# Expert results scattered to the tokens' places tile by tile, and register loads moved and taken one at a time

## What is computed

```python
logits = x @ gate_w + gate_b
probs = jax.nn.softmax(logits, axis=-1)
topv, topi = jax.lax.top_k(probs, K)
topv = topv / jnp.sum(topv, axis=-1, keepdims=True)
comb = jnp.sum(topv[..., None] * jax.nn.one_hot(topi, E, dtype=x.dtype), axis=2)
h = jax.nn.gelu(jnp.einsum('bnd,edf->bnef', x, w1) + b1)
y = jnp.einsum('bnef,efd->bned', h, w2) + b2
ffn_out = jnp.einsum('bne,bned->bnd', comb, y)
return ffn_out + bk_scale * spec_out
```

## Time and profile before

| what | value |
|---|---|
| time, median of 3 runs | 229.34 us (228.66, 229.34, 230.13) |
| the profiled execution | 229.1 us |
| its span, first to last instruction | 227.2 us |
| around the span | 1.9 us |
| mean granted TensorE clock | 0.852 of 2.4 GHz |
| busy: TensorE, VectorE, ScalarE, GpSimd | 161.9, 102.2, 47.6, 75.2 us |
| stretch to 97.5, 97.5 to 123.6, 123.6 to 204.95, 204.95 to 227.2: TensorE busy | 77.8, 2.0, 80.9, 1.2 us |

### The profile page before, as it was taken

How to read it: one execution, slowest core, us unless ns; L and a number is a source line. 1 busy time by engine, 2 the same in 40 slices (tenths; PEclk the granted TensorE clock), 3 DMA queues, 4 the chain that set the end, 5 groups by cost and what they waited for, 6 DMA issues and landing times.

```text
span 227.2 us, 2861 instructions
## 1 busy us (share of the span) xinstructions
PE 161.9 (71%) x928; PEld 133.6 (59%) x928; DVE 102.2 (45%) x302; ACT 47.6 (21%) x89; POOL 75.2 (33%) x196
## 2 busy tenths in 40 slices
PE   0999998888888827610212999999999999993000
PEld 0677754455555415610102899999999999992000
DVE  1129994998899494472103122222332222203445
ACT  0353344343111203210000111232111231110000
POOL 1799300000000121027668877882000000004761
PEclk9999999999999965555555699999999999997555
DMA  6990499999990000003265001000000000011222
GB/s 217 331 408 13 116 265 261 250 261 257 272 341 22 0 1 0 0 0 117 82 197 186 0 5 33 18 19 20 17 31 24 17 20 17 17 38 44 77 56 80
DMA packets 14932, 23.46 MB, mean 103 GB/s; under 512 B 1599, under 2 KB 11396, under 8 KB 14790
## 3 DMA queue, kind: packets, MB, share of 16 engines
q1 hardware_dynamic: 12800, 19.80, 29.9%
q0 software_dynamic: 928, 2.09, 3.0%
q10 hardware_dynamic: 1190, 1.38, 1.9%
HBM read 17.96 MB, written 5.31 MB: 102 GB/s over the span
## 4 chain that ended last, share of the span: by engine, by line
PE 65%; DVE 11%; issue 9%; POOL 5%; DVEq 4%; DMA 3%; ACT 1%; POOLq 0%
PE ps L965 20%; PE ps L975 14%; PE ps L814 8%; PE ps L822 7%; PE ps L823 5%; PE ps L868 4%; POOL diag_s L398 4%; DVEq L746 4%; PE ps L802 3%; DMA w1t_s<-in_w1t 2%; DVE conv L570 1%; DVE stats L616 1%; DVE conv L582 1%; POOL rstd L378 1%; DVE zt L647 1%
## 5 line engine op out<-in xcount | busy, mean ns | idle before, releaser
L965 PE MATMUL ps<-conv 128*128 128x128 f32 x384 | 48.2, 285 | 6.9 <-DVE conv L751 6.5
L965 PEld LDWEIGHTS ps<-conv 128*128 128x128 f32 x384 | 47.3, 201 | 7.6 <-issue 6.8
L570 DVE SCALAR_TENSOR_TENSOR conv<-conv,vecs 128x240 f32<-128x240 f32 (+1 forms) x94 | 35.9, 444 | 7.3 <-ACT conv L447 6.8
L975 PE MATMUL ps<-w_s,conv 128*128 x192 | 33.7, 326 | 0.0
L760 DVE COPY arena<-ps 128x192 f32<-128x192 f32 x16 | 5.7, 358 | 57.5 <-PE ps L975 57.5
L975 PEld LDWEIGHTS ps<-w_s,conv 128*128 128x128 f32 x192 | 30.9, 190 | 0.0
L398 POOL DMA_INDIRECT diag_s<-slot_results,slots x10 | 9.6, 961 | 54.9 <-DMA slot_results<-arena 52.1
L378 POOL TENSOR_TENSOR rstd<-var,neghalf 128x2 f32<-128x2 f32 (+1 forms) x6 | 4.8, 807 | 62.9 <-DVE var L622 62.9
L507 ACT COPY conv<-ps 128x256 f32<-128x256 f32 x16 | 6.0, 373 | 82.8 <-PE ps L956 82.8
L751 DVE COPY conv<-w_s 128x1536 f32 x16 | 15.2, 957 | 14.5 <-issue 9.5
L822 PE MATMUL ps<-conv,pw_s 128*128 128x288 f32 (+1 forms) x48 | 17.4, 445 | 5.5 <-DVE conv L582 3.8
(11 more groups left out here) (152 smaller groups left out, 185.8 us busy)
## 6 DMA issues: line engine op xcount, KB each, us to landing
w_s<-in_w SPq DMA_DIRECT2D x8, 576.0 KB, 18.1
w_s<-in_w SPq DMA_DIRECT2D x8, 384.0 KB
slot_rows<-zero SPq DMA_DIRECT2D x1, 2048.0 KB, 22.2
arena<-in_x SPq DMA_DIRECT2D x4, 432.0 KB, 9.6
w_s<-in_w SPq DMA_DIRECT2D x8, 192.0 KB
slot_results<-arena SPq DMA_DIRECT2D x16, 96.0 KB, 1.6
pw_s<-in_pw SPq DMA_DIRECT2D x1, 1152.0 KB, 11.5
arena<-slot_rows SPq DMA_DIRECT2D x1, 1024.0 KB, 7.6
```

What stands on the lines that cost most here:

```text
L570: ins = nc.vector.scalar_tensor_tensor(out=o, in0=a, scalar=w, in1=o, op0=ALU.mult, op1=ALU.add)
L965: last = mm(p1_ps[i % 2][:, c * P:(c + 1) * P], w1_cur[:, i % 2, k * F + c * P:k * F + (c + 1) * P], xs[:, i % 2, k * P:(k + 1) * P], star ...
L975: last = mm(y_ps[i % 2], hT[:, i % 2, k * P:(k + 1) * P], w2_flat[:, bass.ds(expert[i] * (FK * D) + k * D, D)], start=(k == 0), stop=(k == ...
```

## The change

The rows that are sent carry the token's place. `ht` becomes the first half of `sent`, ScalarE copies the 192 values into the second, and column 193 holds 1 + 2 x token (first place) or 2 + 2 x token (second). After the slot rows are read back, VectorE makes from that column an index for each slot: the place, or a spare row where the column is zero. GpSimd scatters each result tile with these indices into `slot_results`, which now has a row for each token and place; SyncE's sixteen stores are gone. When all sixteen have landed, five plain loads bring each token tile's pairs of rows (three on SyncE, two on ScalarE, and one that repeats the class token's row), and the ten gathers are gone. VectorE's sixteen register loads go one by one into `stage_w1`; TensorE's sixteen move behind its five transposes.

```diff
@@ tower: tiles @@
-        ht = sb("ht", [P, NT, XW])
+        sent = sb("sent", [P, 2, NT, XW])
+        ht = sent[:, 0]
...
+        def load_y(queue, t):
+            w = min(P, K1 - t * P)
+            row = 1 + 2 * t * P
+            queue.dma_start(yg[0:w, t, :, :],
+                            yd[row:row + 2 * w, :].rearrange("(p c) d -> p c d", c=2)).then_inc(d_yg[t], 16)
@@ SyncE @@
-            for i in range(S):
-                sp.wait_ge(y_rdy, i + 1)
-                sp.dma_start(yd[i * P:(i + 1) * P, :], xg[:, i, 0:D]).then_inc(d_yd, 16)
+            sp.wait_ge(d_yd, 16 * S)
+            for t in (0, 2, NT - 1):
+                load_y(nc.sync, t)
@@ GpSimd @@
-            nc.gpsimd.memset(ht[:, :, D:XW], 0.0).then_inc(padded, 1)
+            nc.gpsimd.memset(sent[:, :, :, D:XW], 0.0).then_inc(padded, 1)
...
-            nc.gpsimd.memset(ht[:, :, D:D + 1], 1.0).then_inc(padded, 1)
+            nc.gpsimd.memset(sent[:, :, :, D:D + 1], 1.0).then_inc(padded, 1)
             nc.gpsimd.memset(combp[:, :, SPEC - 1:SPEC], 1.0).then_inc(padded, 1)
+            pool.wait_ge(d_route, 16)
+            nc.gpsimd.tensor_copy(sent[:, :, :, D + 1],
+                                  route_s[:, R_HOME:R_HOME + 2 * NT].rearrange("p (c t) -> p c t", c=2)).then_inc(padded, 1)
...
-            pool.wait_ge(padded, 5)
+            pool.wait_ge(padded, 6)
             pool.wait_ge(ht_rdy, NT)
+            pool.wait_ge(copied, 1)
             pool.wait_ge(slots_rdy, 2)
             for t in range(NT):
                 w = min(P, K1 - t * P)
                 for c in range(2):
                     nc.gpsimd.indirect_dma_start(
                         out=xd, out_offset=bass.IndirectOffsetOnAxis(ap=slots[0:w, c, t:t + 1], axis=0),
-                        in_=ht[0:w, t, :], in_offset=None).then_inc(d_sent, 16)
+                        in_=sent[0:w, c, t, :], in_offset=None).then_inc(d_sent, 16)
             pool.wait_ge(d_sent, 16 * 2 * NT)
             spectral(pool)
+            pool.wait_ge(home_rdy, 1)
+            for i in range(S):
+                pool.wait_ge(y_rdy, i + 1)
+                nc.gpsimd.indirect_dma_start(
+                    out=yd, out_offset=bass.IndirectOffsetOnAxis(ap=home[:, i:i + 1], axis=0),
+                    in_=xg[:, i, 0:D], in_offset=None).then_inc(d_yd, 16)
             pool.wait_ge(d_yd, 16 * S)
-            for t in range(NT):
-                w = min(P, TOK - t * P)
-                for c in range(2):
-                    nc.gpsimd.indirect_dma_start(
-                        out=yg[0:w, t, c, :], out_offset=None, in_=yd,
-                        in_offset=bass.IndirectOffsetOnAxis(ap=slots[0:w, c, t:t + 1], axis=0)).then_inc(d_yg[t], 16)
@@ ScalarE @@
+            act.wait_ge(ht_rdy, NT)
+            nc.scalar.copy(sent[:, 1, :, 0:D], ht[:, :, 0:D]).then_inc(copied, 1)
+
             act.wait_ge(lg_max, 1)
             nc.scalar.activation(comb[:], lg[:], ACT.Exp).then_inc(lg_exp, 1)
...
+            act.wait_ge(d_yd, 16 * S)
+            row = 1 + 2 * (K1 - 1)
+            act.dma_start(yg[LAST + 1:LAST + B, NT - 1, :, :].rearrange("p c d -> p (c d)"),
+                          yd[row:row + 2, :].rearrange("(o c) d -> o (c d)", o=1).to_broadcast([B - 1, 2 * D])
+                          ).then_inc(d_yg[NT - 1], 16)
+            for t in (1, 3):
+                load_y(nc.scalar, t)
@@ VectorE @@
-            dve.wait_ge(padded, 5)
+            dve.wait_ge(padded, 6)
...
-            expert = [nc.vector.value_load(tile_e[0:1, i:i + 1], min_val=0, max_val=E - 1) for i in range(S)]
 
             def stage_w1(i):
+                expert = nc.vector.value_load(tile_e[0:1, i:i + 1], min_val=0, max_val=E - 1)
                 if i >= 2:
                     dve.wait_ge(p1_mm, i - 1)
                 nc.vector.tensor_copy(w1_cur[:, i % 2, :],
-                                      w1_flat[:, bass.ds(expert[i] * (2 * F), 2 * F)]).then_inc(w1_cur_rdy, 1)
+                                      w1_flat[:, bass.ds(expert * (2 * F), 2 * F)]).then_inc(w1_cur_rdy, 1)
 
             stage_w1(0)
             stage_w1(1)
+            for k in range(len(pieces)):
+                dve.wait_ge(d_xg[k], 16)
+            link(nc.vector.scalar_tensor_tensor(out=home_f[:], in0=xg[:, :, D + 1], scalar=0.0,
+                                                in1=route_s[:, R_SPARE:R_SPARE + S], op0=ALU.is_equal, op1=ALU.mult))
+            nc.vector.tensor_tensor(home[:], home_f[:], xg[:, :, D + 1], ALU.add).then_inc(home_rdy, 1)
...
-                    dve.wait_ge(d_yg[t], 32)
+                    dve.wait_ge(d_yg[t], 16 if t < q else 32)
@@ TensorE @@
-            pe.wait_ge(tile_e_rdy, 1)
-            expert = [nc.tensor.value_load(tile_e[0:1, i:i + 1], min_val=0, max_val=E - 1) for i in range(S)]
-
             pe.wait_ge(comb_rdy, 1)
             for t in range(NT):
                 last = nc.tensor.transpose(combt_ps[:, t * P:(t + 1) * P], combp[:, t, :], id_s[:])
             last.then_inc(combt_mm, 1)
+            pe.wait_ge(tile_e_rdy, 1)
+            expert = [nc.tensor.value_load(tile_e[0:1, i:i + 1], min_val=0, max_val=E - 1) for i in range(S)]
             pe.wait_ge(d_w2, 16 * E)
             pe.wait_ge(combt_rdy, 1)
@@ kernel: the table of places, and the size of slot_results @@
+    token = np.arange(NT * P).reshape(NT, P).T
+    route[:, R_HOME:R_SPARE] = np.concatenate([1 + 2 * token, 2 + 2 * token], 1)
+    route[:, R_SPARE:] = 1 + 2 * K1 + np.arange(S * P).reshape(S, P).T
...
-    yd = nc.dram_tensor("slot_results", (S * P, D), F32, kind="Internal").ap()
+    yd = nc.dram_tensor("slot_results", (1 + 2 * K1 + S * P, D), F32, kind="Internal").ap()
```

More of the change, by code:

```diff
@@ L59 @@
 R_TRI, R_ONE, R_THR, R_IOTA, R_VALID = 0, 2 * P, 3 * P, 3 * P + E * E * NT, 3 * P + E * E * NT + S * (E - 1)
-NROUTE = R_VALID + NT * E
+R_HOME, R_SPARE = R_VALID + NT * E, R_VALID + NT * E + 2 * NT
+NROUTE = R_SPARE + S
 def tower(nc, x, vec, rows, had, w1t, plw, pw, projw, cls, ident, layout, route, w1, b1, w2, b2, outw, xd, yd, out):
@@ L130, in tower @@
         wslot = sb("wslot", [P, 2, NT])
+        home_f = sb("home_f", [P, S])
+        home = sb("home", [P, S], I32)
         warm = sb("warm", [P, 1])
@@ L194, in tower @@
         xf_rdy = sem("xf_rdy")
+        copied = sem("copied")
+        home_rdy = sem("home_rdy")
         lg_mm = sem("lg_mm")
@@ L1080 @@
     valid = np.arange(NT * P).reshape(NT, P).T < K1
-    route[:, R_VALID:] = np.repeat(valid, E, 1)
+    route[:, R_VALID:R_HOME] = np.repeat(valid, E, 1)
+    token = np.arange(NT * P).reshape(NT, P).T
+    route[:, R_HOME:R_SPARE] = np.concatenate([1 + 2 * token, 2 + 2 * token], 1)
+    route[:, R_SPARE:] = 1 + 2 * K1 + np.arange(S * P).reshape(S, P).T
     arrays = {
```

## The result

The changed kernel takes 218.15 us (median of 4 runs, 217.18 to 219.08) beside 229.22 for the kernel before (4 runs, 228.66 to 230.13): a ratio of 0.951, 95% interval 0.946 to 0.957. The forecast was 217.4 with a range of 215.3 to 221.5. The profiled execution took 217.86 us with a span of 216.1, 11.1 less than before.

A forecast was written before the change was run, and what follows sets the result against it. Register loads in series on TensorE and VectorE bound the start, TensorE the loop, ten gathers on GpSimd the tail; gains 6.0 + 5.75 = 11.75 us from 229.1 gave 217.4 us, range 215.3 to 221.5.

The forecast's parts named there:

- Two rows of register loads in series, the slot rows next: Start of the tiles: TensorE's and VectorE's sixteen loads lie end to end; moving them gains 6.0 us, until slot rows bound.
- First product at 117.60: Start of the tiles: first product starts at 117.60 instead of 123.59, released by ScalarE's copy of the slot rows.
- the scatter chain, which the change doesn't shorten: the same ten scatters: Before the tiles: ten scatters into the slot rows, same rows from the same moment, are late next; their length stays unchanged.
- The same happens 6 us earlier, and I cost it at nothing: TensorE's clock: 0.50 until the first product's uninterrupted work, then full; the product's 5.46 us stays, cost nothing.
- VectorE's waits and single loads: VectorE: places 124.4, third copy 126.0, asked for at 128.8; in the loop 1.95 of 4.83 us per tile, free.
- GpSimd's backlog: Loop: scatters wait for the spectral chain's end at 154.7, catch up by 165 at 1.25 us each; costs nothing.
- Tail 16.5 us: Last result to end: 16.5 us instead of 22.25, gain 5.75, with plain loads instead of ten gathers.
- (a): Tail: result loads share transfer engines, land 7.6 us after issue; combines at 209.2, time 222.5; chance 0.10.
- (b): Start of the tiles: doesn't move, loads hold it to 123.6; only the tail gains, time 223.35; chance 0.04.
- (c): TensorE: clock stays at 0.50 for one more tile, 4.83 us more, time 222.2; chance 0.05.
- (d): GpSimd: each scatter waits until the one before has landed, 4.05 us each; time 233.7, slower than before; chance 0.03.

The follow-up runs named there:

- the repeated run: The changed kernel measured once more, unchanged, beside three that differ from it: 218.66 us, ratio 0.954 to the kernel before.
- the kernel that holds all sixteen: The changed kernel with no scatter of results before all sixteen results are ready: 237.95 us, ratio 1.040 to the kernel before.

## Why the prediction was right

- **Two rows of register loads in series, the slot rows next.** Right, and sharper than written: I priced both moves together at 6.0. Either alone gives all of it (5.99 and 6.48 us by the medians), the second was worth nothing here.
- **First product at 117.60.** It was 118.20. The step "the scatter chain, which the change doesn't shorten: the same ten scatters" was too short: VectorE's expert copies now lie beside these scatters and cost 0.4 to 0.5 us; 0.1 was already there when the slots were ready. I had read the slowed GpSimd operation of the earlier trace rows, and applied it to the scatters of results alone, where there is slack. There is none for the scatters into the slot rows, and those beside a copy took 1.11, 1.28 and 1.81 us instead of 0.96. By the Trainium skill, SBUF — State Buffer, section Who interferes with whom, a VectorE copy in a two-port mode and a GpSimd instruction exclude each other for a whole instruction. The traces agree that the two get in each other's way; the lengthening, 0.15, 0.32 and 0.85 us, is only once near the whole 0.96 of a copy.
- **"The same happens 6 us earlier, and I cost it at nothing"** (the clock). The first product took 5.04 us, not 5.46, and gave 0.4 back. Two errors of half a microsecond cancelled, which was luck: the second product began at 123.92, forecast 123.84. In the repeated run the first product took 5.48 us and nothing was given back.
- **VectorE's waits and single loads.** Right: places 124.84 (124.4), third copy ready 126.77 (126.0), taken at 128.88 (128.8). A single load cost 0.40 us of VectorE's time and none of the loop's, 75.12 us with single loads and without.
- **GpSimd's backlog.** Right in kind and place: spectral chain done at 155.3 (154.7), queue gone before 168.5 (165), scatters up to 1.97 us apart beside expert copies (159.44 to 161.41; bound 2.2). Holding them back until ten tiles were ready cost nothing. (The spacing of the gathers, for which the prediction names, stands in the earlier trace rows.)
- **Tail 16.5 us.** 16.9 in the profiled execution, 16.6 in six of the eight other runs with this way back (the one that holds all sixteen left aside); the other two had 16.7 and 16.9. The terms: landing of the last scatter seen 2.33 after its start (2.3), first combine at 204.40 (204.05), a wait before the second pair of 0.52 (0.25; it was 0.28 in the repeated run), pairs and statistics as said.
- **Rivals.** The loads sharing and coming late (a): combines at 204.4, not 209.2. The start not moving (b): out. The clock one tile longer (c): out. Each scatter waiting for the former to land (d): they start 1.27 apart. What a queue of scatters costs when it does stand at the end is seen in the kernel that holds all sixteen, 237.95.

Forecast 11.75 and found 11.1 by the profiles; 0.4 of the difference is the tail, 0.15 the loop, 0.1 the start. The loop's 0.15 and 0.3 of the tail's are of the profiled execution alone: in the repeated run the stretches were 75.12 and 16.6.

## What to carry to other kernels

When two engines each issue a row of register loads and one waits for the other, look which resource is due next, and when: here either row could have stayed, and undoing one of them tells more than undoing both. An indirect transfer on GpSimd cost about 1.27 us of its queue here, so sixteen scatters beside the tiles were worth more than ten gathers at the end, though only the last scatter had to be prompt. When a step is moved to an earlier time, ask what it now lies beside: a wide copy on VectorE lengthened the GpSimd scatters that had become the bound.

## What the runs showed of the hardware that was not expected

- The clock's rise isn't at a fixed distance from the start of the first product. In the kernel that held the results' scatters until ten tiles were ready (an edit that touches nothing near 118 us) the product started at 117.67 and took 4.69 us. The slice of TensorE's clock from 121 to 122 us in that kernel:

```profile
121.00:122.00 1.00, 1.00 (x10) 0.82 1.02 356
```

In the kernel before it took 5.46, in the repeated run of the changed kernel 5.48, in the kernel with the loads alone changed 4.63. That is up to 0.8 us by nothing that was edited, more than the effects that the last experiments looked for. What decides it stays open.
- The stretch ahead varies too: between the nine traces that have the changed kernel's code up to there, the subtraction that makes the second slots starts anywhere from 99.02 to 100.30 us. So effects of half a microsecond were read from distances within a trace, not from times of the start or of the whole.
- A scatter of 128 rows on GpSimd takes 0.96 us and 0.30 to the next, and up to 1.81 beside a VectorE copy of 1536 columns; the copies took 0.96 us in the mean before and 0.98 in the changed kernel (one 1.14), so it is nearly all GpSimd that pays.
- A read of 192 KB in rows of 1,536 bytes let VectorE go on 2.6 us after its issue with the five other transfers beside it (201.79 to 204.40), and 2.8 with one that was issued at the same moment (201.66 to 204.43): holding back the transfers behind it didn't bring it sooner.
